# Routed rows of a mixture of experts: 21 tiles of two halves become 18 tiles, ten of two halves and eight of four quarters

## The reference, cut to what matters

```
scores = softmax(xt @ gate_w.T)                     # E = 15 experts
topk_w, topk_idx = top_k(scores, 3); topk_w /= sum
h = einsum('td,efd->etf', xt, fc1_w) + fc1_b        # 2F = 512 columns
a = gelu(h[..., F:]) * h[..., :F] * geglu_mult
y = einsum('te,etd->td', comb, einsum('etf,edf->etd', a, fc2_w) + fc2_b)
out = layernorm(h0 + layernorm_in + y + shared expert of width 512)
```

## Time and profile before

| | |
|---|---|
| median of 3 runs | 211.94 us (211.17 to 212.26) |
| the profiled execution | 211.57 us |
| its span, first to last instruction | 209.8 us |
| PE busy | 199.2 us, 95% |
| DVE busy | 113.2 us, 54% |
| ACT busy | 94.4 us, 45% |
| POOL busy | 121.5 us, 58% |
| TensorE clock granted, mean | 0.992 |

### The profile page before, as it was taken

The page is one execution under the profiler, slowest core; times in us unless marked ns, Lnnn a source line. Parts: engine busy times, 40 slices in busy tenths (PEclk is TensorE's granted clock), DMA queues, the critical chain, the costliest instruction groups (busy, mean ns, idle before and its releaser), DMA issues.

```text
span 209.8 us, 4431 instructions
## 1 busy us (share of the span) xinstructions
PE 199.2 (95%) x1559; PEld 124.7 (59%) x1559; DVE 113.2 (54%) x313; ACT 94.4 (45%) x219; POOL 121.5 (58%) x148
## 2 busy tenths in 40 slices
PE   7999998999998899999998999999999999999981
PEld 4776676678786675776775753355444555445630
DVE  6685697868863444264799953642344332231034
ACT  2004565477868373564557762333332433235024
POOL 0040079869989857929999877216665552347100
PEclk9999999999999999999999999999999999999996
DMA  6999999960000399922220034228985321112483
GB/s 199 391 416 314 402 415 417 425 270 0 6 3 3 97 379 376 417 83 64 78 71 22 0 100 108 78 92 304 366 326 164 92 75 53 50 50 91 145 248 116
DMA packets 13822, 38.32 MB, mean 183 GB/s; under 512 B 2697, under 2 KB 4618, under 8 KB 13802
## 3 DMA queue, kind: packets, MB, share of 16 engines
q1 hardware_dynamic: 11786, 32.54, 42.4%
q0 software_dynamic: 2016, 5.51, 8.4%
HBM read 29.27 MB, written 4.06 MB: 159 GB/s over the span
## 4 chain that ended last, share of the span: by engine, by line
PE 77%; DVE 8%; DMA 6%; issue 2%; ACT 2%; POOL 2%; SPq 1%; POOLq 0%; DVEq 0%; ACTq 0%
PE ps L383 66%; PE ps L1874 3%; PE ps L1672 2%; DMA wres<-y_dram 2%; PE ps L1914 2%; PE ps L1687 2%; DMA embed_sb<-embed 1%; POOL y_dram L668 1%; DMA embed_sb<-x_dram,gather_i 1%; DMA y_dram<-ln_mem,dest_i 1%; PE ps L1603 1%; PE ps L1530 1%; DVE over L1270 1%; POOL embed_sb L659 1%; ACT ln_mem L905 1%
## 5 line engine op out<-in xcount | busy, mean ns | idle before, releaser
L383 PE MATMUL ps<-wres,cT 128*64 (+1 forms) x360 | 63.1, 469 | 0.0
L383 PEld LDWEIGHTS ps<-wres,cT 128*64 128x64 f32 (+1 forms) x360 | 25.4, 131 | 27.7 <-issue 20.5
L668 POOL DMA_INDIRECT y_dram<-ln_mem,dest_i x21 | 20.6, 982 | 26.8 <-ACT ln_mem L875 23.4
L426 POOL TENSOR_TENSOR wres<-wres,fac_mem 128x512 f32<-128x512 f32 x22 | 27.2, 1271 | 4.3 <-DVE ln_rs L1033 4.3
L659 POOL DMA_INDIRECT embed_sb<-x_dram,gather_i x21 | 20.3, 968 | 8.2 <-issue 5.2
L1406 DVE TENSOR_TENSOR fac_mem<-ps,h 128x256 f32<-128x256 f32 x21 | 8.9, 423 | 24.0 <-ACT h L869 24.0
L869 ACT ACTIVATE h<-ps 128x256 f32<-128x256 f32 x21 | 8.0, 383 | 28.5 <-PE ps L383 28.5
L383 PE MATMUL ps<-h,stage 128*128 128x296 f32 x64 | 18.2, 422 | 0.7 <-DVE xn L1384 0.6
L1413 DVE COPY cT<-ps 128x256 f32<-128x256 f32 x21 | 8.8, 424 | 15.6 <-PE ps L383 15.6
L875 ACT ACTIVATE ln_mem<-ps 128x256 f32<-128x256 f32 x21 | 8.0, 383 | 15.8 <-PE ps L383 15.8
L383 PEld LDWEIGHTS ps<-h,stage 128*128 128x128 f32 x64 | 11.6, 190 | 5.4 <-DVE xn L1384 1.0
(11 more groups left out here) (215 smaller groups left out, 379.9 us busy)
## 6 DMA issues: line engine op xcount, KB each, us to landing
wres<-experts SPq DMA_DIRECT2D x15, 768.0 KB, 13.5
fac_mem<-experts SPq DMA_DIRECT2D x11, 256.0 KB, 8.1
wres<-ut SPq DMA_DIRECT2D x3, 768.0 KB, 8.8
embed_sb<-embed SPq DMA_DIRECT2D x5, 416.0 KB, 5.6
stage<-shared SPq DMA_DIRECT2D x2, 771.0 KB, 16.4
stage<-wres SPq DMA_DIRECT2D x2, 512.0 KB
wres<-y_dram SPq DMA_DIRECT2D x2, 512.0 KB, 4.2
wres<-y_dram SPq DMA_DIRECT2D x2, 384.0 KB, 6.3
```

What stands on the lines that cost most here:

```text
L383: return nc.tensor.matmul(o, w, x, start=start, stop=stop)
L426: nc.gpsimd.tensor_tensor(w1(e, c), w1(e, c), row, ALU.subtract).then_inc(less_done, 1)
L668: pool.indirect_dma_start(out=y_dram[:, :], out_offset=bass.IndirectOffsetOnAxis(ap=dest_i[:, column(i):column(i) + 1], axis=0), in_=ys[:, ...
```

## The change

Tiles of four quarters of TQ = 32 rows are added. With quarters the rows need 55 + 15 = 70 quarters, NT = 18 tiles of 128. Ten tiles have two halves: the lower one by register, the upper one with copied weights. Eight have four quarters: 15 free ones (for each expert the odd quarter left over, and what is over in halves; one by register and the rest copied), and 15 that belong to an expert fixed at build time, in four tiles that need no register and no copy. Those four are worked first (`COLUMNS`). There are 21 copies. SP makes every second one by DMA; DVE makes the others with `tensor_copy`, in three instructions each, after loading the expert's number into a register of its own. The copies go through 6 buffers for fc1 and 9 for fc2, which are used again; each copy waits for the tile that used its buffer, and each tile for its own copies. The places in the routing are computed with a second level (half or odd quarter); the owners of quarters are computed after unit 7. SP's writes of `combT` move from before the copies to after the second. The end of PE's order is written out for an even number of tiles.

```diff
-TM = 64
-PT = P // TM
-NT = ((T * TOPK - E) // TM + E + PT - 1) // PT
+TM, TQ = 64, 32
+PT, PQ = P // TM, P // TQ
+QUARTERS = (T * TOPK - E) // TQ + E
+NT = (QUARTERS + PQ - 1) // PQ
+NX = 10
+NHX = PT * NX
+NB = max(QUARTERS - E - PQ * NX, E)
...
+COLUMNS = (14, 15, 16, 17, 0, 1, 10, 2, 3, 11, 4, 5, 12, 6, 7, 13, 8, 9)
+def _parts(n):
+    if n < NX:
+        return [(slice(0, TM), REGISTER, PT * n), (slice(TM, P), COPIED, PT * n + 1)]
+    out = []
+    for h in range(PQ):
+        k = PQ * (n - NX) + h
+        kind = FIXED if k >= NB else COPIED if h else REGISTER
+        out.append((slice(TQ * h, TQ * (h + 1)), kind, NHX + k if k < NB else min(k - NB, E - 1)))
+    return out
+PARTS = [_parts(n) for n in COLUMNS]
+COPIES = [(i, of) for i, parts in enumerate(PARTS) for _, kind, of in parts if kind == COPIED]
+W1_BUFS, W2_BUFS = 6, 9
+DVE_FIRST = ((0,), (1,), (2, 3), (4,), (5,), (6, 7), (8,), (9,), ())
+DVE_SECOND = ((), (), (0,), (1, 2), (3,), (4,), (5, 6), (7, 8), (9,))
...
 (SP)
-            for k in range(NCOPY):
-                e = sp.value_load(owner_i[0:1, NT + k:NT + k + 1], min_val=0, max_val=E - 1)
-                sp.wait_ge(f1_mm, 2 * k + 1)
-                sp.dma_start(copy_w1[k], wres[:, bass.ds(e * WC, W1C)]).then_inc(ld_copy, 16)
-                sp.dma_start(copy_w2[k], wres[:, bass.ds(e * WC + W1C, W2C)]).then_inc(ld_copy, 16)
+            def copy_first(m):
+                c = 2 * m
+                of = COPIES[c][1]
+                copied[m] = sp.value_load(owner_i[0:1, of:of + 1], min_val=0, max_val=E - 1)
+                if c >= W1_BUFS:
+                    sp.wait_ge(f1_mm, COPIES[c - W1_BUFS][0] + 1)
+                sp.dma_start(copy_w1[c % W1_BUFS], wres[:, bass.ds(copied[m] * WC, W1C)]).then_inc(ld_cw1[m % W1_SEMS], 16)
...
+            for m in range(by_dma):
+                copy_first(m)
+                if m:
+                    copy_second(m - 1)
+                if m == 1:
+                    sp.wait_ge(comb_done, 2)
+                    for q in range(4):
+                        rows = comb_dram.rearrange("e (t q c) -> e t q c", q=4, c=32)[:, :, q, :]
+                        sp.dma_start(rows, combT[32 * q:32 * q + NE, :, :]).then_inc(st_comb, 16)
...
 (DVE)
+            def first_copied(m):
+                c = 2 * m + 1
+                of = COPIES[c][1]
+                if m == 0:
+                    dve.wait_ge(own_done, 2)
+                    all_scaled(dve)
+                e = dve.value_load(owner_i[0:1, of:of + 1], min_val=0, max_val=E - 1)
+                dve.wait_ge(f1_mm, COPIES[c - W1_BUFS][0] + 1 if c >= W1_BUFS else 1)
+                for k in range(DC):
+                    nc.vector.tensor_copy(copy_w1[c % W1_BUFS][:, k * 2 * F:(k + 1) * 2 * F], w1(e, k)).then_inc(cw1_done, 1)
+                odd[m] = e
+            def second_copied(m):
+                c = 2 * m + 1
+                if c >= W2_BUFS:
+                    dve.wait_ge(y2_mm, COPIES[c - W2_BUFS][0] + 1)
+                nc.vector.tensor_copy(copy_w2[c % W2_BUFS], wres[:, bass.ds(odd[m] * WC + W1C, W2C)]).then_inc(cw2_done, 1)
             for j in range(0, NT, 2):
                 for i in range(j, min(j + 2, NT)):
                     gated(i)
                 for i in range(max(j - 2, 0), j):
                     gated_in(i)
+                copies(j // 2)
                 if j == 0:
                     softmax_end()
                     weigh()
...
 (PE)
             def weights_1(i, c):
-                yield slice(0, TM), w1(lower[i], c)
-                yield slice(TM, P), w1(i, c) if i < E else copy_w1[i - E][:, c * 2 * F:(c + 1) * 2 * F]
+                for rows, kind, of in PARTS[i]:
+                    if kind == COPIED:
+                        yield rows, copy_w1[COPY_OF[of] % W1_BUFS][:, c * 2 * F:(c + 1) * 2 * F]
+                    else:
+                        yield rows, w1(lower[i] if kind == REGISTER else of, c)
...
-            gated_transposed(NT - 1)
-            second(NT - 3)
+            second(NT - 4)
+            gated_transposed(NT - 2)
+            second(NT - 3)
+            gated_transposed(NT - 1)
             second(NT - 2)
             second(NT - 1)
```

More of the change, by code:

```diff
@@ L252, in vit_tower_kernel @@
         low_bits = sb("low_bits", [P, TOPK * TT], I32)
-        tm_t = sb("tm_t", [P, TOPK * TT])
         start_t = sb("start_t", [P, TOPK * TT])
[L255 to L258, removed]
+        owner_f = sb("owner_f", [P, NHX + NB])
+        owner_i = sb("owner_i", [P, NHX + NB], I32)
+        wrap = sb("wrap", [P, NB])
         tab = sb("tab", [P, 3, NT])
@@ L889, in _ @@
                     tile_out(i)
-            for i in range(NT - 3, NT):
+            for i in range(NT - 4, NT):
                 tile_out(i)
@@ L1254, in reduce_pick @@
                                         AX.X, ALU.add).then_inc(done, 1)
+            counts, upto, before, ends = (over[:, i:i + 2] for i in (0, 2, 4, 6))
+            far, odd_far, least = (over[:, i] for i in (8, 9, 10))
             def slots():
-                held, extra, upto, before, far = (over[:, i] for i in range(5))
                 posn = ps[:, 3, 0:(TT + 1) * E]
+                places = posn[:, 0:TT * E].rearrange("p (t e) -> p t e", t=TT)
                 dve.wait_ge(pos_mm, 1)
-                nc.vector.tensor_scalar(over_i[:, :], posn[:, TT * E:], float(TM - 1), None, ALU.add).then_inc(rt, 1)
-                nc.vector.tensor_tensor(slot[:, :].rearrange("p (t e) -> p t e", t=TT),
-                                        posn[:, 0:TT * E].rearrange("p (t e) -> p t e", t=TT),
+                nc.vector.tensor_scalar(over_i[:, 0], posn[:, TT * E:], 1.0, -1.0, ALU.max, ALU.add).then_inc(rt, 1)
+                nc.vector.tensor_tensor(slot[:, :].rearrange("p (t e) -> p t e", t=TT), places,
                                         rte[:, C_128E:C_128E + E].unsqueeze(1).to_broadcast([P, TT, E]),
@@ L1278, in slots @@
+                nc.vector.scalar_tensor_tensor(far, before[:, 0], float(TM), rte[:, C_CA:C_CA + E],
                                                ALU.mult, ALU.add).then_inc(rt, 1)
-                dve.wait_ge(rt, 8)
+                nc.vector.scalar_tensor_tensor(odd_far, upto[:, 0], -2.0, before[:, 1], ALU.mult, ALU.add).then_inc(rt, 1)
+                dve.wait_ge(rt, 13)
                 nc.vector.scalar_tensor_tensor(
-                    jump[:, :].rearrange("p (t e) -> p t e", t=TT),
-                    posn[:, 0:TT * E].rearrange("p (t e) -> p t e", t=TT), TM - 0.5,
+                    jump[:, :].rearrange("p (t e) -> p t e", t=TT), places, TQ - 0.5,
@@ L1376, in routing @@
                     softmax_start()
+                if k == 7:
+                    owners_copied()
             def unit(k, u, e, n):
@@ L1451, in _ @@
                         mixing_last(k)
+            gated_in(NT - 2)
             gated_in(NT - 1)
```

206 lines of the change are left out of this document (134 added, 72 removed).

## The result

| | kernel before | changed kernel | ratio (95%) |
|---|---|---|---|
| median, us | 211.9 (20 runs, 211.2 to 213.8 and one of 288.8) | 213.9 (20 runs, 211.9 to 216.9) | 1.0071 (1.004 to 1.0101) |
| profiled execution, us | 211.57, span 209.8 | 216.92, span 215.1 | |

The change makes the kernel 0.7% slower; the forecast was 204.5 us and 0.93 for faster.

The account below looks back on a forecast made before the run. TensorE was taken to bound the 21 tiles at 3.165 us each; -9.4 (tiles) + 0.4 (routing) + 1.05 (copies) + 0.55 (tail) = -7.4 gave 204.2 us against the profile's 211.57, 204.5 against the median, range 202.8 to 208.8.

Parts of the forecast that it names:

- copies 13 and 19: VectorE's copies after a turn's last gated_in, wanted by the next turn's first tile 1.7 us later: stalls of 0.2 us each.
- The copy time: One VectorE copy of 512 inside SBUF priced at 0.69 us, from a copy of 512 out of PSUM.
- the fullest turn: VectorE's copies in a turn with two firsts and one second: at most 5.4 us added per pair of tiles.
- Three tiles fewer: PE's tile stage: a quarter tile costs 3.165 us like a half tile, so three fewer save 9.5; -9.4 with the ending.
- one change at the end: PE's new ending parts one pair of transposes: one more change of array mode, about 0.1 us.
- Rival 1: PE's quarter tiles pack worse than halves, at 1.30 of the array time: +6.4, 210.9 us; chance 0.06.
- Stalls by copies: PE's waits around tiles 4, 6, 12 and 16 for copies or work they delay: together +1.05 us, from 0 to 4.
- The tail: After PE's last products the last six scatters follow each other on POOL, instead of five: +0.55 us.
- The routing chain: VectorE's routing work ahead of the tiles, 105 to 118 us, grows by 0.4 us; bounds -0.5 to +2.5.
- Rival 3: VectorE becomes the bound in the tile stage because each copy waits for POOL: +21, 225 us; chance 0.04.
- Rival 2: SP's weight copies 4, 8, 14, 16 and 18 come late by owner load, issue and landing: +3, 207.5 us; chance 0.16.

Follow-up runs that it names:

- e15: The kernel before, nothing edited, one execution on the chip of e14 and e16: 211.46 us, span 209.6.
- e14: Changed kernel with VectorE's copies ahead of gated_in and SP's combine writes one weight copy later; 204.38 us, 0.9663 of the kernel before.
- e16: The kernel of e14 without VectorE's ten copies, PE reading a fixed expert's weights instead: 203.75 us, 0.9622 of the kernel before.
- e5: The changed kernel, nothing edited, timed again on another chip: 214.16 us against 211.91 for the kernel before, ratio 1.0101.
- e4: Changed kernel plus eight products of a zero tile on PE ahead of its waits at tiles 9, 12 and 16: 216.43 us, 1.0107 of the kernel before.
- e18: The kernel of e4 timed again in another job: 216.38 us, 1.0077 of the kernel before.

## Why the prediction was wrong

**The step that failed** is in its part on the copies: "copies 13 and 19 are made after the last gated_in of a turn and wanted by the next turn's first tile, 1.7 us later: 0.2 each". The prediction took the 1.7 us as the time from the last gated_in to the tile's first(). The last gated_in of a turn can't begin until PE has done the last second() of that turn, and after it PE wants the next first() at once. gated_in(9) ends 0.5 us after PE has run out of work. The time left is none; the owner's load, its registers and two copies (1.35 us from 164.71 to 166.06) and gated_in itself are all stall. The rows had it: VectorE's 21 copies L1413 have 15.6 us of idle time in front of them, released by PE's L383. I read there what a copy out of PSUM costs and not that VectorE stands waiting for second() in front of it. The sentence that PE asks for a gated tile 3.7 us after it could be ready is right for gated() in the kernel before; in the changed one two gated() come 0.42 and 0.50 us late. Nothing was asked for gated_in, behind which the diff puts the copies. What this step put at 0.2 us each measured 2.25 and 1.88, and tile 9, whose copy has the same place, 1.09 where the sum had nothing.

**The copy time** of 0.69 us was too high: two copies of 512 take 0.76 us, single ones 0.42. (The 5.4 us for the fullest turn doesn't follow from the prediction's own prices either: five copies of 0.69 and two loads of 0.6 are 4.65.) The rule of the Trainium skill, "VectorE: DVE Perf Modes" (perf-mode tier table: fp32 inside SBUF at twice the rate), from which 0.35 was estimated, is nearer. That should have shrunk the stalls. It did not, since they are made by the position.

**The terms, on one chip.** e15 is the kernel before, e14 the changed kernel without the two late positions, e16 e14 without VectorE's copies. The predicted span difference is -7.4, e15 to e14 is 209.6 to 202.5, -7.1; 204.4 us was measured where 204.5 was forecast. That is luck, since three terms were off and cancel:
- Three tiles fewer, -9.4. Where quarters follow halves or halves quarters, the step is longer, and there are many such changes. In e14's PE timeline the last product of a second() of quarters and the first two of a second() of halves:
```profile
159.22 0.38 PE L419 MATMUL ps<-wres,cT 128*32 x1
...
159.55 0.43 PE L419 MATMUL ps<-wres,cT 128*64 x1
...
159.81 0.38 PE L419 MATMUL ps<-wres,cT 128*64 x1
```
  0.33 us from one form to the other where 0.22 separate products of one form, and 0.26 to the next. In e16, where no copy of VectorE is waited for, the starts of the transposes of the pairs are
```profile
150.84 0.66 PE L1990 MATMUL ps<-cst_sb,embed_sb 128*128 128x128 f32 x4
...
157.19 0.66 PE L1990 MATMUL ps<-cst_sb,embed_sb 128*128 128x128 f32 x4
...
163.96 0.66 PE L1990 MATMUL ps<-cst_sb,embed_sb 128*128 128x128 f32 x4
...
170.72 0.66 PE L1990 MATMUL ps<-cst_sb,embed_sb 128*128 128x128 f32 x4
```
  6.35 apart, where all weight products between are halves, and then 6.77 and 6.76, with three changes of form in each. From 132.97 to 170.72, six intervals, it is 37.75; e15 has 36.28 for its six (132.70 to 168.98). Of the difference 1.3 us fall to the four intervals with changes, nine in all, 0.14 us each; nearly all of the rest is in the first, which has none. With the changes outside these marks they cost some 1.5 us. The prediction had 0.1 for one change at the end, a figure without a row. Rival 1, quarters that pack worse at 1.30, is wrong all the same.
- Stalls by copies, +1.05: between the same marks e14 takes 38.30, 0.55 over e16.
- The tail, +0.55: the last scatter starts 1.57 us behind ScalarE's last read in e14 and 1.75 in e15, so -0.2. The first of the last run of six starts 4.8 us before that read, not 4.1:
```profile
180.12 0.97 POOL L725 DMA_INDIRECT y_dram<-ln_mem,dest_i  x1 [3.66 <-ACT ln_mem L932]
...
186.50 0.97 POOL L725 DMA_INDIRECT y_dram<-ln_mem,dest_i  x1 [0.31 <-issue]
```
```profile
184.93 0.38 ACT L932 ACTIVATE ln_mem<-ps 128x256 f32<-128x256 f32 x1 [0.48 <-PE ps L419]
```
- The routing chain, +0.4: 0.33 by the first gather (118.98 in e15, 119.31 in e14), with the two waits for POOL of 1.0 us at the places that were named.

**The changed kernel against 204.5.** The waits of PE in its profile from 130 us to tile 16 (0.44, 0.69, 0.42, 1.09, 0.17, 2.25, 0.50, 1.88) are 7.4 us, 6.4 over the term. With +1.4 for the changes of form and -0.75 for the tail that makes 211.6; the runs with the higher clock have 212.7, and the 1.1 us between are not accounted for. The median is 213.9 with the others, whose clock is lower. In the profiled execution that is 1.7 us at tile 12 and as much at the end, where the last sums take 3.77 us and not the 2.10 of the earlier trace rows (granted clock 0.88 over 200 to 210 us). Beside that, the last read of y_dram takes 6.13 us, against 4.75 in the kernel before and 4.47 in e5:
```profile
200.09 6.13 DMA wres<-y_dram
```
That the clock falls because of the waits is argued from their order in the trace. The runs with products in the waits (e4, e18) have it at 0.983 to 0.996 and were not faster by ratio, so how much it is worth in the median stays open.

**The rivals.** Rival 3, the one that ended slower, named the wrong mechanism: no copy waits for POOL (the longest of the 30 lasts 0.63 us). Rival 2 put SP's copies late; SP had one late copy, worth 0.69 us. That VectorE's copies are late by position was in the forecast as two tenths of a microsecond each and had no rival of its own.

## What to carry to other kernels

When work is put behind an instruction, read what that instruction waits for, not when it usually ends: copies placed behind a step that is itself released by PE's last product of the turn can only begin when PE has already run dry. The profile shows it in the idle time before the neighbour, and in its releaser. When a form that packs as well as another is mixed with it, count the changes of form too, and where two variants were timed on different chips, put them on one before their difference is explained.

## What the runs showed of the hardware

- After a wait of PE of 2.25 us the steps of four quarters were 0.85 us apart and not 0.43, the granted clock at its lower level (1.2 GHz), for the next 3.5 us in one execution (0.83 over the window) and not in another (1.00).
- A load of one value into VectorE's registers and the arithmetic on it leave VectorE idle for 0.33 us (tile 16), 0.59 (tile 12) and 1.19 (tile 9) in front of the copies; the two copies of 512 behind them take 0.76.
- Four quarters over 512 elements, register-addressed and copied blocks mixed, take 0.43 us a step, the same as two halves; a change between the two forms costs 0.11 us at the change (0.33 for 0.22) and 0.04 at the step behind it (0.26 for 0.22), 0.14 by the intervals of e16.
- In three of the six jobs the chip ran the kernel before 2.0 to 3.4 us slower, at the same mean granted clock (0.979 to 0.997 on one kind, 0.985 to 0.997 on the other), and every trace taken there has the late signal at the first tile.
